# Two units' weighted values in one run, and an output bank opened by transpositions, in a fused attention and MLP kernel

## The reference

```python
x = rmsnorm(tokens, attn_norm_w) * (1.0 + 0.1 * tanh(scale)) + shift
q, k, v = split(x @ qkv_w.T + qkv_b);  q, k = rope(q), rope(k)
tokens = tokens + merge_heads(softmax(q k^T / sqrt(8), valid) v) @ out_w.T + out_b
cq = rmsnorm(tokens, sq_norm_w) @ wq.T + bq;  ck, cv = rmsnorm(seq_tokens, s_norm_w) @ (wk, wv).T + (bk, bv)
update = (merge_heads(softmax(cq ck^T / sqrt(8), svalid) cv) @ mha_out_w.T + mha_out_b) * valid_rows
tokens = tokens + sigmoid([tokens, update] @ gate_w.T + gate_b) * update
g, val = split(rmsnorm(tokens, ffn_norm_w) @ gu_w.T + gu_b)
return tokens + silu(g) * val @ down_w.T + down_b
```

## Time and profile before

| what | value |
|---|---|
| median of 3 runs | 512.85 us (512.27 to 514.27) |
| the profiled execution's own time | 517.94 us |
| its span | 516.1 us |
| PE busy | 442.1 us, 86% |
| DVE busy | 350.1 us, 68% |
| ACT busy | 290.4 us, 56% |
| POOL busy | 190.8 us, 37% |
| mean granted TensorE clock | 0.937 of 2.4 GHz |

### The profile page before, as it was taken

How to read it: one execution, slowest core, us unless ns; L and a number is a source line. 1 busy time by engine, 2 the same in 40 slices (tenths; PEclk the granted TensorE clock), 3 DMA queues, 4 the chain that set the end, 5 groups by cost and what they waited for, 6 DMA issues and landing times.

```text
span 516.1 us, 13226 instructions
## 1 busy us (share of the span) xinstructions
PE 442.1 (86%) x5219; PEld 308.3 (60%) x5219; DVE 350.1 (68%) x655; ACT 290.4 (56%) x644; POOL 190.8 (37%) x184
## 2 busy tenths in 40 slices
PE   3546889878897986999989988999999969999897
PEld 2115375756675664666577655866586748565664
DVE  2326655878885896698677866767748856856565
ACT  4321364577566664777576648486636744556243
POOL 4451140614433163528381828254542542000010
PEclk9975778899997999799999999999989999999999
DMA  3355442354353445344443443425140320000001
GB/s 77 87 174 174 131 122 88 100 162 151 100 162 107 140 121 153 103 128 121 131 137 108 117 140 97 153 67 163 43 149 25 98 92 3 23 3 22 22 1 42
DMA packets 62942, 52.04 MB, mean 101 GB/s; under 512 B 3803, under 2 KB 61728, under 8 KB 62880
## 3 DMA queue, kind: packets, MB, share of 16 engines
q1 hardware_dynamic: 60050, 49.07, 32.2%
q10 hardware_dynamic: 2830, 2.12, 1.4%
HBM read 8.55 MB, written 2.11 MB: 21 GB/s over the span
## 4 chain that ended last, share of the span: by engine, by line
PE 52%; DVE 11%; DMA 10%; ACT 8%; issue 8%; SPq 5%; POOL 4%; ACTq 1%; DVEq 0%; POOLq 0%
PE ps_o L403 8%; PE ps_a L366 7%; PE ps_g L320 7%; PE ps_b L386 6%; PE ps_g L461 5%; SPq L658 4%; DMA k_st<-part_k 4%; DVE top L1087 4%; PE ps_g L444 4%; PE ps_g L353 3%; DMA q_st<-top_t 3%; ACT probs L902 2%; DMA s_in<-in_fside_BxSxS 1%; ACT turned_in L838 1%; PE ps_g L418 1%
## 5 line engine op out<-in xcount | busy, mean ns | idle before, releaser
L1087 DVE TENSOR_REDUCE top<-ps_a 128x4 f32<-128x512 f32 x256 | 169.6, 680 | 106.1 <-PE ps_a L366 104.8
L902 ACT ACTIVATE probs<-ps_b 128x512 f32<-128x512 f32 x256 | 151.3, 595 | 143.6 <-PE ps_b L386 139.5
L366 PE MATMUL ps_a<-k_st,q_st 73*128 73x128 bf16 x1024 | 105.0, 228 | 27.8 <-DMA k_st<-part_k 15.0
L366 PEld LDWEIGHTS ps_a<-k_st,q_st 73*128 73x128 bf16 x1024 | 69.8, 101 | 79.5 <-issue 59.9
L386 PE MATMUL ps_b<-q_st,k_st 75*128 75x128 bf16 x1024 | 102.0, 223 | 9.4 <-ACT probs L902 7.5
L386 PEld LDWEIGHTS ps_b<-q_st,k_st 75*128 75x128 bf16 x1024 | 69.6, 99 | 18.5 <-issue 9.2
L403 PE MATMUL ps_o<-probs,v_pad 128*32 128x128 f32 x2048 | 73.3, 287 | 0.0
L403 PEld LDWEIGHTS ps_o<-probs,v_pad 128*32 128x32 f32 x2048 | 55.3, 115 | 24.1 <-issue 14.7
L728 POOL TENSOR_TENSOR f<-f 128x4 f32<-128x4 f32 x16 | 16.6, 1038 | 98.8 <-DVE f L1136 98.8
L320 PE MATMUL ps_g<-norm,w_t 128*128 128x512 f32 x66 | 37.1, 647 | 1.2 <-DVE hid L1178 1.2
L320 PE MATMUL ps_g<-turned_in,w_t 128*128 128x512 f32 x48 | 30.3, 717 | 5.0 <-ACT turned_in L838 4.8
(11 more groups left out here) (197 smaller groups left out, 677.6 us busy)
## 6 DMA issues: line engine op xcount, KB each, us to landing
q_st<-part_q SPq DMA_DIRECT2D x126, 128.0 KB
k_st<-part_k SPq DMA_DIRECT2D x120, 128.0 KB
x_in<-in_x SPq DMA_DIRECT2D x16, 256.0 KB, 4.5
q_st<-hid SPq DMA_DIRECT2D x18, 128.0 KB
s_in<-in_fside_BxSxS SPq DMA_DIRECT2D x8, 256.0 KB, 5.7
out<-t SPq DMA_DIRECT2D x8, 256.0 KB, 2.3
k_st<-hid SPq DMA_DIRECT2D x12, 128.0 KB
swap_q<-part_q SPq DMA_DIRECT2D x8, 128.0 KB, 2.3
```

The source lines that it names most:

```text
L366: mm = pe.matmul(ps_a[q % 2][:, j * S:(j + 1) * S], st[0][i][0:R_MAX, h, b * S:(b + 1) * S], st[1][i][0:R_MAX, h, b * S:(b + 1) * S], star ...
L902: act.activation(probs[:, n % 2, q * T:(q + 1) * T], ps_b[q % 2][:, :], ACT.Exp, scale=SCALE).then_inc(exp_done, 1)
L1087: dve.tensor_reduce(top[:, n // 2 % 2, n % 2, QH * q:QH * (q + 1)], ps_a[q % 2][:, :].rearrange("p (h k) -> p h k", h=QH), AX.X, ALU.max). ...
```

## The change

The weighs of both units of a pair move to one place, position 1 of the next pair: weigh(n - 2), then weigh(n - 1). The even unit's weigh so comes three steps later and the odd unit's one step earlier. Since the even slot of probs is then read later, ACT's first exponential of each even unit moves from position 0 to position 1, where two exponentials follow each other. DVE's take_pair and divide_pair each move one step earlier. In out_product the bank is opened by four transpositions (the identity moving through the array in transposition mode) where it was closed by four identity products, the product with out_w comes last, and the wait for x_in comes ahead of all of them.

```diff
             def out_product(g, t):
 
+                pe.wait_ge(x_loaded, 16 * (x_load[CROSS, g] + 1))
                 pe.wait_ge(att_set, 2 * POS[SELF, g] + 2)
                 to, done = take(("out", g), t, 3, 2)
-                pe.matmul(to[:, :], w_t[:, W_OUT, :], att_s[g % 3][:, :], start=True, stop=False)
-                pe.wait_ge(x_loaded, 16 * (x_load[CROSS, g] + 1))
                 for b in range(NG):
-                    mm = pe.matmul(to[:, b * S:(b + 1) * S], x_in[:, b, :], ident[:, :], start=False, stop=b == NG - 1)
-                mm.then_inc(done, 1)
+                    pe.matmul(to[:, b * S:(b + 1) * S], x_in[:, b, :], ident[:, :], is_transpose=True,
+                              start=b == 0, stop=False)
+                pe.matmul(to[:, :], w_t[:, W_OUT, :], att_s[g % 3][:, :], start=False, stop=True).then_inc(done, 1)
...
-                if q == 2 and 0 <= n - 1 < UNITS:
+                if n % 2 == 0 and q == 1 and 0 <= n - 2 < UNITS:
+                    weigh(n - 2)
                     weigh(n - 1)
...
-                if 0 <= n < UNITS:
+                if 0 <= n < UNITS and (n % 2 == 1 or q > 0):
+                    if n % 2 == 0 and q == 1:
+                        exps(n, 0)
                     exps(n, q)
...
-                if n % 2 == 0 and q == 3 and 0 <= (n - 2) // 2 < PAIRS:
+                if n % 2 == 0 and q == 2 and 0 <= (n - 2) // 2 < PAIRS:
                     take_pair((n - 2) // 2)
-                if n % 2 == 1 and q == 1 and 0 <= (n - 3) // 2 < PAIRS:
+                if n % 2 == 1 and q == 0 and 0 <= (n - 3) // 2 < PAIRS:
                     divide_pair((n - 3) // 2)
```

## The result

The changed kernel took 527.6 us (median of 4 runs, 521.27 to 532.62) where the kernel before took 512.56 in the same session. The ratio is 1.0179, 95% interval 1.0119 to 1.0238: slower, where 506.4 us was forecast. Timed again later, the changed kernel was at 1.0214 (1.016 to 1.0268). The profiled execution took 523.97 us, with a span of 522.2 and a mean granted clock of 0.914 of 2.4 GHz, where before had 517.94, 516.1 and 0.937.

What follows compares the result with a forecast made beforehand. PE was taken as the bound on average (86% busy), though the chain ran only 52% on it. Terms -5.3 + 2.4 + 0.6 - 2.6 - 1.5 = -6.4 us from 512.85 gave 506.4 us, range 500.5 to 513.5.

Steps and rivals of the forecast that it cites:

- Where the weighs stand on the chain: Count of weighs on the last-ending chain: 37.4 instead of 39, taking 37.6 us instead of 42.9.
- 5.3 us less: Saving on the chain from paired weighs at position 1: 42.9 us before, 37.6 after.
- 2.4 back: Loss set against the saving: some 12 weighs leave the chain, 0.2 us taken off for each.
- (c): Rival: PE comes 1.1 us early to position 0 waits and pays both weighs behind; 509.4 to 515.4 us, chance 0.29.
- (d): Rival: early arrival at waits decides everywhere, DVE and ACT lacking slack at position 6; over 0.5% slower, chance 0.07.
- bound of 13.2 us for the departures: Upper bound of the loss if all 12 weighs leaving the chain save nothing, at 1.1 us each.
- So it costs nothing: ACT's even-unit first exponential, waiting for the first weigh: 1.6 us of cover for 0.6 us of work, cost zero.
- The clock: Rival: longer position 0 waits bring two or three more half-speed stretches, about 1.5 us each; 509.5 to 511, chance 0.02.
- signs of being wrong: PE waiting for exponentials at position 2 or x_in, DVE waits growing over 5 us, or mean clock below 0.93.
- The out product: Transpositions replace identity products: 1.36 us instead of 1.80 with out_w; six of eight groups on the chain, 2.6 us less.
- the wait for k_st: PE's waits for the stacks' DMAs: still three, each longer by up to 1 us.
- The end: After the last weigh, half a down projection covers four DVE steps, 2.24 us for 2.1; 1.5 us less counted.

Runs made afterwards that it cites:

- nothing is held: First exponential back at position 0: with weighs at positions 0 and 1, 1.0029; with both weighs at position 1 and a second buffer for it, 1.0283 of before.
- the weighs apart: Changed kernel with the even unit's weigh at position 0, the odd unit's at 1, first exponential at position 0: 1.0029 of before; exponential at position 1: 1.0172.
- the run in the tail alone: Kernel before with the new out product, and both weighs together only for the last two pairs (units 60 to 63): 508.49 us, 0.9883 of before.

## Why the prediction was wrong

**The step that failed is "Where the weighs stand on the chain".** It counted 18.7 of 32 runs on the chain of before and held that chain fixed; 27 of 32 are on it, which in the prediction's own terms is 27 x 2.01 = 54.3 us in place of 37.6. The chain of before left PE at positions that weighs had kept busy. With both weighs at position 1 the score groups at positions 2 to 7 have 2.2 us less of PE's work between them, and DVE and ACT, which stood still during the run, set the pace there: behind 24 of the 27 runs the chain goes to DVE or ACT within 2 us and comes back at positions 3 to 7 or 0. The saving was real on PE and bought nothing, since the weighs no longer lay under DVE's and ACT's work. The 5.3 us less and 2.4 back became a loss. That moving the weighs and what goes with them costs about 3% is shown by the parts (1.0297 with the old out product; 1.0179 and 1.0214 against 0.991 with the new). What the run itself costs depends on the rest: 2.5 to 2.9% where nothing is held (1.0029 and 1.0283, 0.9982 and 1.0268), nothing measurable where the exponential is held in both (1.0172 against 1.0179 and 1.0214). How the loss splits between DVE's pace, ACT's pace and the waits at position 0 was read from single places only, and stays open.

**Rival (c) and (d) had the mechanism** (PE comes early to a wait and pays for both weighs behind it), as 313.92 to 318.62 shows at one place, but I gave (d) only 0.07. The argument against it, DVE's 68% of busy time and 1.02 us idle at one place, was an average and a single gap; what counted was DVE's and ACT's load in the six steps between runs. The bound of 13.2 us for the departures was in the text and left out of the range; even with it the sum gives 517.3, so the departures alone, as they were priced, don't reach the 521 to 533 measured.

**DVE's move was never costed.** The prediction gave no term to take_pair and divide_pair one step earlier. With the weighs at positions 2 and 6 they cost 2.5% (0.991 to 1.0158). It also passed over the wait that they lengthen: it calls 15.0 and 7.5 us the two largest entries of PE's waits, but the second largest was that for DVE's maxima, 7.7 us in 15. In the run of two they cost nothing and even help: with the old steps 1.0344, with the new 1.0179 and 1.0214; with nothing held 1.0268 and 1.0283, no difference. The effects don't add, and why the old steps are worse in the run with the hold stays open. Its mean clock is lower, 0.910 against 0.921, which names no cause.

**"So it costs nothing", of the held exponential,** was wrong with the weighs apart, where the hold costs 1.4%. The sum looked at PE's next demand for that exponential and not at ACT's other work behind it. By which wait it costs isn't shown: PE's waits by name are nearly the same with and without it (1.73 us for the normalization in both), and what differs is the mean clock, 0.918 against 0.930. In the run of two it can't be called wrong: there nothing was gained without the hold.

**The clock had a chance of 0.02.** It went from a mean of 0.936 to 0.921, some 3 to 6 us. The text priced two or three stretches at half speed of 1.5 us each; the stretch of 130 to 220 us alone has 15 us more at half speed in one profile and 4 in the other. Two of the prediction's own signs of being wrong came true: waits for DVE that grow by more than 5 us (9.2) and a mean clock below 0.93. The rule of the Trainium skill that the prediction weighed (TensorE: Matmul & The Clock Gate, Part 4: transposition mode does not count as work for the clock gate) was not the reason: with the new out product alone the mean clock is 0.936, as before.

**What held.** The out product: forecast 1.36 us and measured 1.30; its gain was put at 2.6 us and came out at 4.6, with an interval of 2.3 to 7.0. The run of two: 1.9 forecast, 1.89 measured. No wait for x_in. The sign of the wait for k_st was wrong: 9.9 us, and 13.4 in the second profile, instead of 15.0.

**The end** was forecast to lose its whole wait, 1.5 us. It kept most of it. The timeline of the changed kernel there:

```profile
489.07 2.05 PE L461 MATMUL ps_g<-w_t,hid 128*128 128x128 f32 x16
489.21 0.72 DVE L1108 STREAM_TRANSPOSE turned<-ps_o 128x512 f32<-128x512 f32 x1 [1.65 <-PE ps_o L403]
489.96 0.35 DVE L1110 RECIPROCAL inverse<-turned 128x32 f32<-128x32 f32 x1
...
491.16 0.69 DVE L1188 TENSOR_TENSOR t<-ps_g,down_bias 128x512 f32<-128x512 f32 x1 [0.85 <-PE ps_g L461]
491.77 0.41 DVE L1120 TENSOR_TENSOR quotient<-turned,inverse 128x256 f32<-128x256 f32 x1
492.22 0.45 DVE L1128 STREAM_TRANSPOSE att_c<-quotient 128x256 f32<-128x256 f32 x1
...
492.72 0.70 PE L320 MATMUL ps_g<-att_c,w_t 128*128 128x512 f32 x1 [1.16 <-DVE att_c L1128]
```

The half down projection that was to cover DVE's four steps made a bank that DVE reads (L1188) between the reciprocal and the quotient. DVE waits 0.85 us for it in the middle of its chain, the four steps take 3.6 us instead of 2.1, and 1.16 us of wait remain of 1.58. The same 0.85 and 1.16 us stand in the kernel with the run in the tail alone. The cover became part of what it covered.

## What to carry to other kernels

Work on the bounding engine that separates groups for its readers is spacing, not only cost: before bunching it, sum what each reader has to do between the bunches and compare it with what the engine leaves it, and don't count the chain of before as if it stayed. Cost every move in a diff, those on an engine with a third of its time free too: here two instructions of 1.05 us in all, one step earlier, stood in front of a reduction that PE needed, and the kernel was 0.9% slower. When several changes are tested, cross them before one is blamed: the hold and the run each cost much where the other was absent and little where it was there. Bunching at the tail, where no maxima are left to reduce, did no harm (0.9883 against 0.991), but a gain from it isn't clear of the noise.

## What the runs showed of the hardware

- Four float32 transpositions of 128 columns took 0.44 us to the next group at full clock (95.25 to 95.69), half of what eight parts of identity products took, and the granted clock of the kernel with them was the same 0.936 on average.
- The granted clock varies from execution to execution of one kernel, 0.915 to 0.950 in 68 executions of the kernel before, and spans go with it, 3.8 us for 0.01 (correlation -0.79; 2.0 us without the ten longest). In the changed kernel 3 to 6 of the 12 us that it is longer go with its lower mean, 0.921.
- After the waits of PE at 336.93 (1.45 us) and 344.05 (1.35 us) the same four parts of L320 took 3.72 us instead of 1.94, at a granted clock of 0.50 (1.2 GHz), though PE had no wait over 1.5 us between the run at 332.51 and there.
